# Attention steps reordered: transposes ahead of scores, a shorter lag, context products in seven pieces, one-step spreading of the row sums

## What is computed

```python
q, k, v = (proj(Wq, bq), proj(Wk, bk), proj(Wv, bv))
scores = jnp.einsum('bhqd,bhkd->bhqk', q, k) * SCALE
mask = (adj_matrix + bond_matrix)[:, None, :, :]
scores = scores * mask
attn = jax.nn.softmax(scores, axis=-1)
ctx = jnp.einsum('bhqk,bhkd->bhqd', attn, v)
...
return jnp.einsum('bse,fe->bsf', ctx, Wo) + bo
```

## Time and profile before

| what | value |
|---|---|
| median of three runs | 3322.37 us |
| profiled execution, its own time | 3321.2 us |
| its span, first to last instruction | 3319.2 us |
| TensorE busy, of the span | 3121.4 us (94%) |
| VectorE busy | 2140.8 us (64%) |
| ScalarE busy | 1728.5 us (52%) |
| GpSimd busy | 403.9 us (12%) |
| mean granted TensorE clock | 0.978 |

### The profile page before, as it was taken

How to read it: one execution, slowest core, us unless ns; L and a number is a source line. 1 busy time by engine, 2 the same in 40 slices (tenths; PEclk the granted TensorE clock), 3 DMA queues, 4 the chain that set the end, 5 groups by cost and what they waited for, 6 DMA issues and landing times.

```text
span 3319.2 us, 69826 instructions
## 1 busy us (share of the span) xinstructions
PE 3121.4 (94%) x27800; PEld 2737.3 (82%) x27800; DVE 2140.8 (64%) x3900; ACT 1728.5 (52%) x3009; POOL 403.9 (12%) x1613
## 2 busy tenths in 40 slices
PE   7999999999999999999989999899998999989998
PEld 6987789877898778987789877898778987789877
DVE  5626876278762786637866378653886538874387
ACT  3425854258442684426844268432784327743377
POOL 0001110011100111001110001100111001110011
PEclk9999999999999999999999999999999999999999
DMA  5112131121321213202133021330213302123110
GB/s 206 46 57 68 42 136 56 50 65 49 128 77 33 63 48 128 92 21 68 40 128 102 12 66 44 124 102 14 65 49 118 102 19 63 56 107 102 33 30 18
DMA packets 145263, 234.41 MB, mean 71 GB/s; under 512 B 12839, under 2 KB 113964, under 8 KB 144940
## 3 DMA queue, kind: packets, MB, share of 16 engines
q1 hardware_dynamic: 144940, 229.96, 21.6%
HBM read 120.86 MB, written 83.89 MB: 62 GB/s over the span
## 4 chain that ended last, share of the span: by engine, by line
PE 83%; DVE 10%; issue 3%; ACT 3%; POOL 1%; SPq 0%; DVEq 0%; DMA 0%; POOLq 0%; ACTq 0%
PE ps L451 15%; PE ps L453 15%; PE ps L452 15%; PE ps L642 14%; PE ps L632 9%; PE ps L657 6%; DVE rsum L1144 2%; PE ps L531 2%; PE ps L585 1%; PE ps L506 1%; PE ps L672 1%; DVE xt_lo L1065 1%; PE ps L520 1%; DVE ev L1216 1%; DVE r L1178 1%
## 5 line engine op out<-in xcount | busy, mean ns | idle before, releaser
L1284 DVE CUSTOM_DVE_ANT_0 r<-ps,adjn 128x1024 f32<-128x1024 f32 x512 | 622.2, 1215 | 14.0 <-PE ps L632 8.3
L1005 ACT ACTIVATE r<-r,nmax 128x1024 f32<-128x1024 f32 x512 | 585.5, 1144 | 81.1 <-POOL nmax L443 81.1
L451 PE MATMUL ps<-u_hi,t_hi 128*128 128x256 f32 x2048 | 589.3, 288 | 6.0 <-DVE u_lo L1058 4.8
L452 PE MATMUL ps<-u_lo,t_hi 128*128 128x256 f32 x2048 | 580.7, 284 | 0.0
L453 PE MATMUL ps<-u_hi,t_lo 128*128 128x256 f32 x2048 | 580.4, 283 | 0.0
L642 PEld LDWEIGHTS ps<-ident,r 128*128 128x128 f32 x4096 | 461.3, 140 | 118.7 <-issue 77.6
L642 PE MATMUL ps<-ident,r 128*128 128x128 f32 x4096 | 537.3, 274 | 4.5 <-DVE pt L1303 3.5
L1303 DVE COPY pt<-ps 128x512 f32<-128x512 f32 x512 | 353.0, 689 | 116.2 <-PE ps L642 110.1
L451 PEld LDWEIGHTS ps<-u_hi,t_hi 128*128 128x128 f32 x2048 | 393.2, 192 | 10.6 <-DVE u_lo L1058 7.1
L452 PEld LDWEIGHTS ps<-u_lo,t_hi 128*128 128x128 f32 x2048 | 394.0, 192 | 0.0
L453 PEld LDWEIGHTS ps<-u_hi,t_lo 128*128 128x128 f32 x2048 | 393.7, 192 | 0.0
(11 more groups left out here) (162 smaller groups left out, 5357.1 us busy)
## 6 DMA issues: line engine op xcount, KB each, us to landing
adjn<-in_adj SPq DMA_DIRECT2D x64, 512.0 KB, 3.7
t_spill<-t_hi SPq DMA_DIRECT2D x64, 512.0 KB, 4.3
t_spill<-t_lo SPq DMA_DIRECT2D x64, 512.0 KB, 5.2
t_hi<-t_spill SPq DMA_DIRECT2D x32, 1024.0 KB, 5.4
t_lo<-t_spill SPq DMA_DIRECT2D x32, 1024.0 KB, 8.0
xn<-in_x SPq DMA_DIRECT2D x16, 512.0 KB, 4.7
x_spill<-xn SPq DMA_DIRECT2D x64, 128.0 KB, 1.7
q_stack<-u_hi SPq DMA_DIRECT2D x64, 128.0 KB, 2.4
```

Source lines behind the costliest of these rows:

```text
L451: pe.matmul(dst, a_hi, b_hi, start=first, stop=False, skip_group_check=check)
L452: pe.matmul(dst, a_hi, b_lo, start=False, stop=False, skip_group_check=check)
L1005: act.activation(r[:, s % RSLOTS, :], r[:, s % RSLOTS, :], ACT.Exp, bias=nmax[:, s % 4:s % 4 + 1], accum_out=prow[:, qt % 2, h:h + 1]).the ...
L1284: dve.tensor_tensor_reduce(out=r[:, s % RSLOTS, :], in0=ps[:, 2 * (s % 2):2 * (s % 2) + 2, :].rearrange("p a c -> p (a c)"), in1=adjn[:, q ...
```

## The change

In TensorE's step the order becomes: T of unit `s-2` (`LAG` is 2), S of unit `s+1`, then the context and the rest. In steps 0 and 1 S stands first and two pairs of value projections follow in each, in place of one pair in each of four steps; VectorE's copies of them move with them.

A group's context is no longer two calls of 32 records. The eight key tiles of the first group come in pieces of 3, 3 and 2 in steps 7, 8 and 9, those of the second in four pieces of 2 in steps 10 to 13, and so on every eight steps; step 14 has none. `pt` is split in halves with rings of their own, 7 slots for the first and 8 for the second; `r` has 3 slots, and two slots of the second half lie in the space of its fourth. A semaphore `ctx_half` says when the first half of a group is used.

`denominators`, `rt` and `sel` go. `spread_denominators` is done in step 11 with eight small matmuls (16 records), each with a column of `rprow` repeated over 32 columns (an operand with step zero) as weights and the identity as the moving operand. The copy to `rbc` moves from step 13 to 12, `c_hi` from 15 to 14, the output from 17 to 16, and `c_lo` from VectorE to GpSimd, except for the last query tile of an element.

```diff
-    LAG = 3
+    LAG = 2
...
-        PSLOTS, RSLOTS = 6, 4
+        RSLOTS, P0SLOTS, P1SLOTS = 3, 7, 8
...
+                    if u >= 16 and (u - 16) % H == 0 and (u - 16) // H < NT - 1:
+
+                        qt = (u - 16) // H
+                        pool.wait_ge(c_hi_ready, nth(b, NT, qt + 1))
+                        pool.tensor_tensor(c_lo[:, :, :], c_f[:, :, :], f32(c_hi[:, :, :]), ALU.subtract).then_inc(c_ready, 1)
...
+            def context(b, grp, kts):
 
                 qt, g = divmod(grp, 2)
-                pe.wait_ge(p_act if part else p_dve, nth(b, UNITS, G * grp + G))
...
+                for kt in kts:
+                    if kt == 0:
+                        pe.wait_ge(p_dve, nth(b, UNITS, G * grp + G))
+                        if grp == 0:
+                            pe.wait_ge(pr_free, nth(b, PR_UNITS, PR_UNITS))
+                        elif g == 0:
+                            pe.wait_ge(c_raw, nth(b, NT, qt))
+                    if kt == TPH:
+                        pe.wait_ge(p_act, nth(b, UNITS, G * grp + G))
...
+            def spread_denominators(b, qt):
+
                 pe.wait_ge(rp_ready, nth(b, NT, qt + 1))
                 if qt >= 1:
                     pe.wait_ge(h_sum, nth(b, NT, qt))
-                pe.matmul(ps[0:H, 7, 0:P], rprow[:, qt % 2, :], ident[:, :], start=True, stop=True).then_inc(rt_full, 1)
-
-            def spread_denominators(b, qt):
-                pe.wait_ge(rt_ready, nth(b, NT, qt + 1))
                 for g in range(2):
-                    last = pe.matmul(ps[:, 7, g * P:(g + 1) * P], sel[:, g, :], rt[:, :], start=True, stop=True)
+                    for hh in range(G):
+                        h = g * G + hh
+                        last = pe.matmul(ps[HD * hh:HD * (hh + 1), 7, g * P:(g + 1) * P],
+                                         rprow[:, qt % 2, h:h + 1].broadcast_to([P, HD]), ident[:, :],
+                                         start=True, stop=True, tile_position=(0, HD * hh))
...
+                PIECES = {7: (0, range(0, 3)), 8: (0, range(3, 6)), 9: (0, range(6, 8)),
+                          10: (1, range(0, 2)), 11: (1, range(2, 4)), 12: (1, range(4, 6)), 13: (1, range(6, 8))}
                 for s in range(UNITS + 10):
-                    if s + 1 < UNITS:
+                    if s + 1 < UNITS and s < LAG:
                         scores(b, s + 1)
-                    if s < PAIRS:
-                        project_pairs(b, "values", W_V, xt_wait(b, 3), range(s, s + 1))
+                        project_pairs(b, "values", W_V, xt_wait(b, 3), range(2 * s, 2 * s + 2))
                     if LAG <= s < UNITS + LAG:
                         transpose_p(b, s - LAG)
...
+                    if s + 1 < UNITS and s >= LAG:
+                        scores(b, s + 1)
+                    for at, (g, kts) in PIECES.items():
+                        if s >= at and (s - at) % H == 0 and (s - at) // H < NT:
+                            context(b, 2 * ((s - at) // H) + g, kts)
                     if s >= 11 and (s - 11) % H == 0 and (s - 11) // H < NT:
...
+                        spread_denominators(b, (s - 11) // H)
+                    if s >= 16 and (s - 16) % H == 0 and (s - 16) // H < NT:
+                        output(b, (s - 16) // H)
```

More of the change, by code:

```diff
@@ L169, in build_program @@
             r = sb("r", [P, RSLOTS, N], F32, s)
+            pt_2 = sb("pt_2", [P, 2, TPH, P], F32, s)
+        with ExitStack() as s:
+            al_area = sb("al_area", [P, 4, N], F32, s)
         with ExitStack() as s:
@@ L185, in build_program, with p_half @@
         f32 = lambda ap: ap.bitcast(F32)
-        al = lambda t: r[:, 1 + t % 3, :]
+        al = lambda t: al_area[:, 1 + t % 3, :]
+        def p_half(u, half):
+            if half == 0:
+                return pt_0[:, u % P0SLOTS, :, :]
+            k = u % P1SLOTS
+            return pt_1[:, k, :, :] if k < P1SLOTS - 2 else pt_2[:, k - (P1SLOTS - 2), :, :]
         set_in = sem("set_in")
@@ L245, in build_program @@
         p_dve = sem("p_dve")
+        ctx_half = sem("ctx_half")
         ctx_done = sem("ctx_done")
         rp_ready = sem("rp_ready")
-        rt_full = sem("rt_full")
-        rt_ready = sem("rt_ready")
         rbc_full = sem("rbc_full")
@@ L398, in _ @@
             pool.memset(zero[:, :], 0.0).then_inc(set_const, 1)
-            pool.wait_ge(set_const, 6)
+            pool.wait_ge(set_const, 5)
             pool.affine_select(out=ident, in_=ident, compare_op=ALU.not_equal, fill=1.0, base=0,
                                pattern=[[-1, P]], channel_multiplier=1).then_inc(set_const, 1)
[L403 to L407, removed]
             def layer_norm(b, layer):
@@ L430, in _ @@
                     layer_norm(b, layer)
-                for u in range(UNITS + 12):
-                    if u >= 19 and (u - 19) % H == 0 and (u - 19) // H < NT:
-                        norm_tile(b, 3, (u - 19) // H)
+                for u in range(UNITS + 13):
+                    if u >= 20 and (u - 20) % H == 0 and (u - 20) // H < NT:
+                        norm_tile(b, 3, (u - 20) // H)
+                    if u >= 16 and (u - 16) % H == 0 and (u - 16) // H < NT - 1:
+                        qt = (u - 16) // H
+                        pool.wait_ge(c_hi_ready, nth(b, NT, qt + 1))
+                        pool.tensor_tensor(c_lo[:, :, :], c_f[:, :, :], f32(c_hi[:, :, :]), ALU.subtract).then_inc(c_ready, 1)
                     if u >= 14 and (u - 14) % H == 0 and (u - 14) // H < NT:
@@ L657, in context @@
                         last = pe.matmul(ps[HD * hh:HD * (hh + 1), 6, g * P:(g + 1) * P],
-                                         xn[:, kt, h * HD:(h + 1) * HD], pt[:, (grp * G + hh) % PSLOTS, kt, :],
+                                         xn[:, kt, h * HD:(h + 1) * HD], p_half(grp * G + hh, kt // TPH)[:, kt % TPH, :],
                                          start=(kt == 0), stop=(kt == NT - 1), tile_position=(0, HD * hh))
-                if part:
-                    last.then_inc(ctx_done, 1)
-            def denominators(b, qt):
+                    if kt == TPH - 1:
+                        last.then_inc(ctx_half, 1)
+                    if kt == NT - 1:
+                        last.then_inc(ctx_done, 1)
+            def spread_denominators(b, qt):
                 pe.wait_ge(rp_ready, nth(b, NT, qt + 1))
@@ L812, in _ @@
             act.wait_ge(set_in, SET_LOADS)
-            act.wait_ge(set_const, 9)
+            act.wait_ge(set_const, 6)
             for n, slot in enumerate((W_L0X, W_L0G, W_Q, W_K, W_V, W_O)):
@@ L995, in _ @@
                         act.wait_ge(p_full, nth(b, 2 * UNITS, 2 * u + 2))
[L996 to L999, removed]
+                        if u >= P1SLOTS:
+                            act.wait_ge(ctx_done, nth(b, 2 * NT, (u - P1SLOTS) // G + 1))
+                        copy(p_half(u, 1).rearrange("p t q -> p (t q)"), ps[:, TP + 1, :]).then_inc(p_act, 1)
                     if s < UNITS:
@@ L1006, in _ @@
                                        accum_out=prow[:, qt % 2, h:h + 1]).then_inc(exp_done, 1)
[L1007 to L1012, removed]
+                    if s >= 12 and (s - 12) % H == 0 and (s - 12) // H < NT:
+                        qt = (s - 12) // H
                         act.wait_ge(rbc_full, nth(b, NT, qt + 1))
@@ L1287, in _ @@
                             accum_out=mmax[:, s % 4:s % 4 + 1]).then_inc(masked, 1)
-                    if s < PAIRS:
-                        n = pr["values", s]
-                        if s == 0:
+                    for k in range(2 * s, 2 * s + 2) if s < LAG else ():
+                        n = pr["values", k]
+                        if k == 0:
                             dve.wait_ge(spilled, nth(b, 16 * NT, 16 * NT))
                         dve.wait_ge(pr_full, nth(b, PR_UNITS, n + 1))
-                        dve.tensor_copy(xn[:, 2 * s:2 * s + 2, :].rearrange("p t f -> p (t f)"),
+                        dve.tensor_copy(xn[:, 2 * k:2 * k + 2, :].rearrange("p t f -> p (t f)"),
                                         ps[:, PR + n % 2, :]).then_inc(pr_free, 1)
@@ L1300, in _ @@
                         dve.wait_ge(p_full, nth(b, 2 * UNITS, 2 * u + 1))
[L1301 to L1304, removed]
+                        if u >= P0SLOTS:
+                            dve.wait_ge(ctx_half, nth(b, 2 * NT, (u - P0SLOTS) // G + 1))
+                        dve.tensor_copy(p_half(u, 0).rearrange("p t q -> p (t q)"), ps[:, TP, :]).then_inc(p_dve, 1)
                     if s >= 8 and (s - 8) % H == 0 and (s - 8) // H < NT:
@@ L1329, in _ @@
                             dve.sem_inc(drained, 1)
-                        tile_stats(b, 3, qt)
+                    if s >= 18 and (s - 18) % H == 0 and (s - 18) // H < NT:
+                        tile_stats(b, 3, (s - 18) // H)
 def kernel(**inputs):
```

39 lines of the change are left out of this document (11 added, 28 removed).

## The result

The changed kernel takes 3297.05 us, the median of five runs (3296.22 to 3305.78), against 3321.77 for the kernel before. The ratio is 0.9934, with a 95% interval of 0.9923 to 0.9946: 0.66% faster. The forecast was 3284. The profiled execution's span is 3294.1 us, 25.1 less than before.

The account below looks back on a forecast made before the run. TensorE was taken to bound the kernel. Per element, seven periods at 0.5 us, 0.4 at the start and 0.9 at the end gain 4.8; eight gain 38, giving a 3284 us median, range 3258 to 3332.

Parts of the forecast that it names:

- What bounds, and the price of a piece: Mid-stage attention: TensorE bounds the period; each context piece costs 0.28 us to get into the array and out.
- The rival on drains: Context pieces: the way in and out costs 0.37 us each, period 18.05 to 18.1, time 3317 us; chance 0.15.
- the slower one: Between S and context: S must end first, 0.44 us a piece, period 18.6, time 3345 us; chance 0.17.
- Row sums: Spreading behind a context piece: 16 records in four rounds, 0.44 us, in place of 1.05; 0.6 gained on TensorE.
- The end of an element: Last contexts to c_f: c_f can start at 442.5 instead of 443.38, 0.9 us less an element.
- The waits before: Kernel before, mid-stage: 0.65 us of waits a period, seen as 0.61 ahead of one S (partly C's way out) and longer T.
- The wait in step 14: Light step 14: the copy tie lets no step be under 1.47 us, costing 0.12 us a period there.
- Start: Start of an element's attention: T of unit 0 after three S instead of five, 0.4 us gained a stage.
- c_lo: c_lo moved to GpSimd: takes 0.37 us a period off VectorE, with no value while TensorE bounds.
- rings: Waits for slots of the pt halves and of r: all at nothing, covered by TensorE's order.
- SyncE queue: Stores on SyncE: the queue keeps its order and waits for the same normalise, half a step earlier or later.
- The shorter lag shows: Steps 15 and 16: exp late, T waits, 0.3 us a period, period 17.8, time 3301 us; chance 0.13.

Follow-up runs that it names:

- the four even pieces: Changed kernel with each group's context in two pieces of four key tiles (steps 7, 9, 11, 13) instead of seven pieces: 3265.79 us, ratio 0.9834.

## Why the prediction was right, and where it wasn't

The time lies in the range and on the forecast side, but the sum was right for half a reason, and that the measured gain comes to 25 us of the 38 is luck: only 11.5 of them come from what I had costed. I take it in its own steps.

*What bounds, and the price of a piece: right.* T behind a context piece is 1.02 to 1.03 and a piece of 16 records 0.57, so 0.15 + 0.57 - 0.44 = 0.28 for the way in and out, the value taken. The steps came out as 2.25, 3.10, 2.01 for the three forecast as 2.29, 2.99, 2.07 (the way out moves from T to the output), then 2.07, 2.51, 2.07, 2.07 as forecast. The rival on drains and the slower one, S having to end first, fall with that. The Trainium skill's rule that a change of tiling mode drains the engine (TensorEngine Tiling (Array Packing), Key Properties) agrees with the gap on either side of each piece. They cost 0.28 a piece and not the 0.37 of that rival, and the four even pieces show what seven visits come to. The idle time of the weight loads would have misled: it is 0.36 to 0.37 ahead of each piece and 0.20 behind it, 0.57 in all, and the matmuls lost half of that.

*Row sums: right,* 0.44. The end of an element, from the last T to c_f, is 0.77 us shorter where 0.9 was said. Of the way there, the forecast had c_f 2.4 us behind the start of the last contexts; it is 2.96 (440.07 to 443.03), since the piece of step 9 stands among them too: 24 rounds, not 20.

*The waits before: one misread.* The 0.61 of issue ahead of the S at 746.16 in the earlier trace rows isn't a way out of C. That S waited for the mask, and it did so in one of the few periods of 18.35 us; in the period behind it the same S waits 0.15:

```profile
746.16 0.74 PE L632 MATMUL ps<-k_stack,q_stack 96*128 96x512 f32 x2 [0.51 <-DVE mmax L1284]
...
764.15 0.73 PE L632 MATMUL ps<-k_stack,q_stack 96*128 96x512 f32 x2 [0.15 <-DVE mmax L1284]
```

The sum didn't use the 0.61.

*The wait in step 14: mis-sized.* I let the next T start after 1.47 us and it is 1.69. I had put the way out of a piece into the piece. It falls on the T behind it, ahead of S, so the S, the mask and the copy of the next unit all come 0.15 to 0.2 later. The timeline of the changed kernel shows the tie:

```profile
766.75 1.23 DVE L1292 CUSTOM_DVE_ANT_0 r<-ps,adjn 128x1024 f32<-128x1024 f32 x1 [0.24 <-PE ps L638]
...
767.90 0.69 DVE L1311 COPY pt<-ps 128x512 f32<-128x512 f32 x1
...
768.70 0.86 PEld L648 LDWEIGHTS ps<-ident,r 128*128 128x128 f32 x8 [0.54 <-ACT r L1017]
768.74 1.06 PE L648 MATMUL ps<-ident,r 128*128 128x128 f32 x8
```

The mask waits 0.24 for the scores; the copy follows it and ends at 768.59; T starts 0.15 behind, about the lag of the earlier trace rows. The load's row names exp as what it waited for, but exp and its sum had been done at 768.13: it was the copy.

With scores first that wait is gone and step 14 is 1.47, as that run showed. So the period is 17.77, not 17.5: 0.23 a period, not 0.5. That term of the sum, 7 x 0.5 an element, should have been 1.2 for the first six periods behind unit 7 (five at 0.23, the first at 0.06), less 0.56 in the last one, where the kernel before, with most scores gone, took 16.54 and the changed one 17.10. I had left both out.

*Start: wrong.* T of unit 0 comes 1.35 us sooner after the first scores (7.11 in place of 8.46), and T of unit 7 gives 1.32 back: 0.03 in place of 0.4. With two pairs of value projections and their copies a step, the mask of unit 2 starts 7.9 us behind the first scores in place of 5.1, and from there to 310.8 us the chain is mostly VectorE's masks and copies.

*c_lo, rings, SyncE queue:* nothing, as said. *The shorter lag shows:* not seen. T of step 15 waits for the copy, not for exp.

In all an element's attention gained 1.2 - 0.56 + 0.03 + 0.77 = 1.44 us where I said 4.8, 11.5 us for all eight in place of 38. The other 1.7 of the measured 13.2 are clock again: in three of the eight elements the kernel before runs the output at 1.2 GHz, 0.63 us longer each, and the changed one in none (in the last, 0.21 us from one matmul to the next, against 0.12). The 12 us outside attention were in no step. Without them the changed kernel would stand at 3297 + 12 = 3309 us (an estimate); the version with c_lo on VectorE, which hasn't got them, stands at 3307, 0.4% faster than before. And the rise that the prediction credited to evenness isn't one: against the new spreading alone, seven pieces, order and lag together cost 0.20 a period. The weakness was to compare the changed schedule only with the one before, and never with its own parts.

## What to carry to other kernels

Cost each part of a bundled change by itself, against the kernel with only the others: here one part brought 0.9% and the rest took some back, and laying the same work in four visits on every other step in place of seven brought 1.0% more. When two shapes of matmul alternate, each visit has a fixed price; spread it as far as the buffers need and no further, and put small work of the same shape behind a visit that is there anyway. Where the bound engine's clock can fall, compare the length and the granted clock of stretches that the change doesn't touch before a gain is put down to the change.

## What the runs showed of the hardware

The stages outside attention, the same instructions in every kernel, took 2041 to 2047 us in eleven profiled executions, 2033.4 in the changed kernel and 2032.5 in it with the idle time filled, and 2038.3 with scores first. The granted clock differs with them. Taken by element (without the first), the stretch takes 253.4 to 253.7 us where 10.2 us of it are at 1.2 GHz (14 of them), 254.7 to 256.4 where 17.1 are (53) and 257.3 to 257.9 where 20.5 are (10). So the 12 us go with time at the lower level. A difference of 10 us came back in a second profile of the same kernel (c_lo on VectorE: 2047.0 and 2045.9), so it goes with the kernel, and not only with the execution. What in the kernel decides it isn't settled: filling the idle time at the end of attention left the sum at the lower level where it was, 136.8 us for 136.5. It stays open.

A stationary operand of one column repeated with step zero, 32 wide, cost no more than a plain one: 16 records in 0.44 us, four beside each other, the same 0.11 a round that the context's come to.
